# DLRM tower with a two-layer CIN on one core: the third bank's products as 32 matmuls of 32 columns and 8 of 4 in place of 8 of 132

## The reference, cut to what matters

```python
e = jnp.stack([tbl_f[ids[:, f]] for f in range(32)], axis=1)      # 1024 x 32 x 32
x = e
for W in (W0, W1):                                                # 1024 x 128, 4096 x 128
    z = jnp.einsum('bhd,bmd->bhmd', e, x).reshape(b, n * prev, k)
    x = jnp.einsum('bpd,pj->bjd', z, W)
    res.append(x)
z = jnp.sum(jnp.concatenate(res, axis=1), axis=-1)                # 1024 x 256
h = relu(concat([z, dense_ctx]) @ W_top1 + b_top1)
y = relu(h @ W_top2 + b_top2) @ W_top3
```

## Time and profile before

| | |
|---|---|
| median of the runs shown | 376.89 us |
| span of the profiled execution | 597.7 us |
| one tile after the last gather (527.5 to 563.8) | 36.3 us |
| last stretch (563.8 to 597.7) | 33.9 us |
| TensorE passes and weight loads | 3656 and 3656 |
| granted TensorE clock, whole span | 0.800 |

### The profile page before, as it was taken

The page is one execution under the profiler, slowest core; times in us unless marked ns, Lnnn a source line. Parts: engine busy times, 40 slices in busy tenths (PEclk is TensorE's granted clock), DMA queues, the critical chain, the costliest instruction groups (busy, mean ns, idle before and its releaser), DMA issues.

```text
span 597.7 us, 9512 instructions
## 1 busy us (share of the span) xinstructions
PE 412.6 (69%) x3656; PEld 360.8 (60%) x3656; DVE 203.4 (34%) x834; ACT 235.5 (39%) x774; POOL 246.5 (41%) x262
## 2 busy tenths in 40 slices
PE   5512112874257887877788778687787679999988
PEld 4301001653256776766666667577676668989988
DVE  4200000694723333322333233333332235556510
ACT  3300000662175334522343334433452237676641
POOL 6777772547055444544445554544444440000000
PEclk9755555795589877877787888977787779999999
DMA  8100000000000000000000000000000000000000
GB/s 299 45 14 13 13 13 6 11 3 14 2 10 10 8 10 7 10 8 9 9 9 10 10 10 9 11 8 9 8 10 8 8 10 2 2 2 2 2 2 1
DMA packets 10765, 9.66 MB, mean 16 GB/s; under 512 B 4664, under 2 KB 8896, under 8 KB 10720
## 3 DMA queue, kind: packets, MB, share of 16 engines
q0 software_dynamic: 8192, 4.21, 4.8%
q1 hardware_dynamic: 2528, 4.84, 2.3%
HBM read 9.03 MB, written 0.00 MB: 15 GB/s over the span
## 4 chain that ended last, share of the span: by engine, by line
PE 57%; issue 18%; another core or an unknown queue 11%; DVE 7%; ACT 6%; DMA 1%; SPq 0%; ACTq 0%
PE WA L725 20%; PE QB L697 10%; PE PA L687 8%; PE T L710 4%; DVE RT L421 4%; PE M L738 4%; PE M L757 2%; PE ET L674 2%; ACT eblk L285 2%; ACT TS L285 1%; PE PA L639 1%; PE M L764 1%; PE M L748 1%; ACT RT L285 1%
## 5 line engine op out<-in xcount | busy, mean ns | idle before, releaser
L278 POOL DMA_INDIRECT emb<-in_table,rows x256 | 245.8, 960 | 239.0 <-PE ET L674 165.3
L725 PE MATMUL WA<-TS,RX 128*128 128x128 f32 x896 | 127.0, 301 | 1.0 <-ACT TS L285 1.0
L584 DVE COPY TS<-T 32x64 f32<-32x64 f32 x256 | 55.5, 217 | 200.6 <-PE T L710 184.6
L725 PEld LDWEIGHTS WA<-TS,RX 128*128 128x128 f32 x896 | 119.7, 215 | 6.0 <-issue 6.0
L697 PE MATMUL QB<-eblk,zQ 128*64 128x68 f32 x1024 | 69.1, 243 | 74.3 <-issue 74.0
L697 PEld LDWEIGHTS QB<-eblk,zQ 128*64 128x64 f32 x1024 | 49.9, 146 | 89.8 <-issue 85.8
L552 DVE TENSOR_TENSOR zQ<-ET,eT 128x1024 f32<-128x1024 f32 x32 | 39.2, 1225 | 159.0 <-ACT eT L285 158.9
L687 PE MATMUL PA<-eblk,zP 128*128 128x132 f32 x512 | 80.6, 296 | 5.3 <-issue 3.4
L639 PE MATMUL PA<-sym,TS 128*128 128x272 f32 x64 | 29.4, 552 | 74.5 <-issue 47.3
L687 PEld LDWEIGHTS PA<-eblk,zP 128*128 128x128 f32 x512 | 73.4, 212 | 6.3 <-issue 4.9
L285 ACT ACTIVATE eblk<-ET 32x256 f32<-32x256 f32 x128 | 48.6, 380 | 71.0 <-PE ET L674 66.0
(11 more groups left out here) (87 smaller groups left out, 294.1 us busy)
## 6 DMA issues: line engine op xcount, KB each, us to landing
emb<-in_table,rows POOLq DMA_INDIRECT x256
TS<-in_W SPq DMA_DIRECT2D x8, 256.0 KB, 4.3
wt<-in_W_top SPq DMA_DIRECT2D x2, 512.0 KB
y1w<-in_W_rows SPq DMA_DIRECT2D x1, 448.0 KB
TS<-in_W_rows SPq DMA_DIRECT2D x1, 448.0 KB
sym<-in_W_cols SPq DMA_DIRECT2D x1, 264.0 KB, 2.8
TS<-in_W_cols SPq DMA_DIRECT2D x1, 264.0 KB, 3.1
idc<-in_ids SPq DMA_DIRECT2D x1, 128.0 KB, 2.0
```

Source lines behind the costliest of these rows:

```text
L278: eng.indirect_dma_start(emb[par][:, g, :], None, table, bass.IndirectOffsetOnAxis(rows[:, k, g:g + 1], 0))\
L584: eng.tensor_copy(view(ts[32 * q:32 * q + 32, :, :], P * REST + b0, [[4 * P, 2], [P, 4], [1, 8]]), view(src, q, [[C17, 2], [4, 4], [C33, 8 ...
L725: m = eng.matmul(WA[:, 0:P], C[:, kt, :], TS[k % 2][:, slot_of(kt), :], start=(kt == 0), stop=(kt == KT - 1))
```

## The change

`other_triples` now runs per group `g` four matmuls, one for each `q`: the same weights `z3[:, g, :]`, and from `eblk` only the fields with index `q` modulo 4 (32 columns: 4 samples, 2 halves, 4 fields, which lie 4 elements apart). The result goes to partitions `32q` of `T3`, columns `32g` on. Then 8 matmuls of 4 columns each (the inner column of ones) go to partitions 0 to 31. So `T3` already has the partitions of `TS`, and ScalarE brings it there with one copy of 128 x 256 and one of 32 x 32, in slot 1 of the next unit. VectorE's `rest_copies` and the semaphore `t3_also` go.

```diff
-            def rest_copies(u, j):
+            def rest_copies(u):
                 k, unit = divmod(u, UNITS)
-                b0 = 32 * unit + 8 * j
-                src = T3[32 * j:32 * j + 32, :]
+                b0 = 32 * unit
                 eng.wait_ge(t3_made, u + 1)
-                for q in range(NQ):
-                    copy(view(TS[k % 2][32 * q:32 * q + 32, :, :], P * REST + b0, [[4 * P, 2], [P, 4], [1, 8]]),
-                         view(src, q, [[C17, 2], [4, 4], [C33, 8]])).then_inc(t3_also, 1)
-                copy(TS[k % 2][0:32, REST1, b0:b0 + 8], view(src, ONES, [[C33, 8]])).then_inc(t3_also, 1)
+                copy(view(TS[k % 2][:, :, :], P * REST + b0, [[P, 8], [1, 32]]),
+                     view(T3[:, :], 0, [[1, 8], [8, 32]])).then_inc(t3_kept, 1)
+                copy(TS[k % 2][0:32, REST1, b0:b0 + 32], T3[0:32, 8 * 32:9 * 32]).then_inc(t3_kept, 1)
...
-                if r < 2 and u > 0:
-                    rest_copies(u - 1, r + 2)
+                if r == 1 and u > 0:
+                    rest_copies(u - 1)
...
             for u in range(ALL):
-                if u > 0:
-                    for part in range(3):
-                        rest_copies(u - 1, part)
...
             def other_triples(u):
-                wait(eng, t3_kept, 10 * u)
-                wait(eng, t3_also, 10 * u)
-                for x in range(2):
-                    for j in range(NQ):
-                        g = 2 * j + x
-                        at = NQ * C33 * x
-                        m = eng.matmul(T3[32 * j:32 * j + 32, at:at + NQ * C33].rearrange("p (v c) -> p v c", c=C33),
-                                       z3[u % 2][:, g, :], eblk[u % 2][:, g, :, 1:], start=True, stop=True)
+                wait(eng, t3_kept, 2 * u)
+                for g in range(GROUPS):
+                    for q in range(NQ):
+                        some = view(eblk[u % 2][:, :, :, :], EB * g + 1 + q, [[2 * C17, NQ], [C17, 2], [NQ, NQ]])
+                        eng.matmul(T3[32 * q:32 * q + 32, 32 * g:32 * g + 32].rearrange("p (v a b) -> p v a b", v=NQ, a=2),
+                                   z3[u % 2][:, g, :], some, start=True, stop=True)
+                for g in range(GROUPS):
+                    m = eng.matmul(T3[0:32, 8 * 32 + NQ * g:8 * 32 + NQ * g + NQ], z3[u % 2][:, g, :],
+                                   eblk[u % 2][:, g, :, C17], start=True, stop=True)
                 m.then_inc(t3_made, 1)
```

More of the change, by code:

```diff
@@ L173, in dlrm_cin_tower @@
         t3_kept = sem("t3_kept")
-        t3_also = sem("t3_also")
         y2_made = sem("y2_made")
@@ L406, in _ @@
             across_copy(ALL - 1)
-            for j in range(2, NQ):
-                rest_copies(ALL - 1, j)
+            rest_copies(ALL - 1)
             y1_copy(END)
@@ L568, in products @@
                        .then_inc(z_made, 1)
[L570 to L587, removed]
             eng.wait_ge(ids_loaded, 16 * 2)
@@ L620, in _ @@
                     late_sums(u)
-            for part in range(3):
-                rest_copies(ALL - 1, part)
             eng.wait_ge(tower_loaded, 16 * 5)
@@ L721, in second @@
                 if pieces[-1] >= F + HALF:
-                    eng.wait_ge(t3_kept, 10 * UNITS * (k + 1))
-                    eng.wait_ge(t3_also, 10 * UNITS * (k + 1))
+                    eng.wait_ge(t3_kept, 2 * UNITS * (k + 1))
                 for kt in pieces:
```

## The result

The changed kernel takes 384.12 us (median of 4 runs, 383.88 to 384.72) against 376.88 us before (4 runs, 376.80 to 377.10). The ratio is 1.0191, with a 95% interval of 1.0173 to 1.0210: 7.2 us slower. The forecast was 382.0 us, in a range of 375 to 396.

The account below looks back on a forecast made before the run. TensorE was taken as the bound, at 36.3 us a tile. The third bank's added +14.8 us and the -9.4 us from removed copies summed to +5.4 us, 382 us, in a range of 375 to 396.

Parts of the forecast that it names:

- the tile of 36.3 us: The stretch after the gathers, with TensorE busy 34.95 us, taken as each tile's cost; eight make 290 us.
- The third bank, +0.51 us a unit: The T3 matmuls on TensorE were to take 1.09 us in place of 0.58, at 30 ns a pass.
- +14.8: Added TensorE time in us for the T3 matmuls: 0.51 us in each of 29 units.
- The relief, -9.4 us: Time off the path because VectorE's and ScalarE's copies of T3 no longer delay TensorE: 4.7, 1.1 and 3.6 us.
- (1): First tile: two batches of ten VectorE copies ahead of the sums TensorE awaits go, -4.7 us (0 to 4.7).
- (2): First tile: ScalarE's copies of the folded table no longer wait behind five T3 copies, -1.1 us (0 to 2.2).
- (3): Later tiles: the towers' ReLUs no longer stand behind T3 copies on ScalarE, 0.6 us in six tiles, -3.6 us.
- the gathers' pace: Rival: GpSimd's gathers, one per 1.24 us, hide both cost and relief; +1.0 us, 378 us, chance 0.17.
- the columns that lie apart: Rival: moved columns 4 elements apart take twice the time, 56 ns a pass; +17.6 us, 394 us, chance 0.12.
- Issue's pace: Rival: issuing sets the third bank's time at 36 ns a pass; +57 us, 434 us, chance 0.10.
- Faster, under 24 ns a pass: Rival: third-bank passes are cheap enough for the relief to win; at 20 ns a pass 373 us, chance 0.13.
- L757's wait of 0.55 us: Sign in the changed kernel's profile: TensorE's wait for the towers' ReLUs is 0.55 us, in place of 1.35.

Follow-up runs that it names:

- the second profile: The kernel before, unchanged, profiled once more: span 375.7 us, median 377.5 us (1 run).
- the gathers' cover off: Half the gathers from the third tile on: before 369.0 us, changed kernel 383.9 us, before's matmuls with the changed kernel's two copies 354.9 us.

## Why the prediction was right in sign and size, and where it was wrong

**"TensorE is the bound"** holds for the changed kernel (80% of its chain) and failed for the one before, from some 240 us on. The step that failed is the tile of 36.3 us, taken for "what every tile costs". Dropping the 74.0 us of waits as the recorder's was right: the second profile has no such wait. But a tile with gathers takes at least 32 x 1.25 us = 40 us in the end, and that stood in the earlier trace rows beside the 36.3 of the earlier trace rows. I compared the end of all gathers (322 us) with the time and found 14 us to spare. Those 14 us were not there: in the second profile the last gather ends at 333.3, 11.3 us later, its landing takes 1.5 more, and 1.8 lie outside the span. The gathers are late because several of the first take twice as long:

```profile
43.80 2.12 POOL L278 DMA_INDIRECT emb<-in_table,rows  x1 [0.30 <-issue]
...
54.99 0.94 POOL L278 DMA_INDIRECT emb<-in_table,rows  x1 [0.30 <-issue]
...
38.95 6.36 DVE L421 TENSOR_TENSOR RT<-RT,RX 128x64 f32<-128x64 f32 x25
```

The slow ones fall where VectorE adds from and to SBUF; that VectorE is their cause was not tried.

**The third bank, +0.51 us a unit.** It is +0.97, and the step that failed is the price of a 32-column pass, 30 ns by the rule "of weights or of what is moved, whichever is more". That is nearly right for columns side by side (34 ns for four passes in four tiles, bank 1.13 us), and the 4-column passes cost what was forecast (0.59 us for 16 with the change of shape, against 0.61). Columns 16 bytes apart take 60 ns. That was a rival, at 56 ns with +0.93 a unit and a chance of 0.12, and it is shown by three steps of spacing. The +14.8 should have been +29.0.

**The relief, -9.4 us.** With the gathers' cover off it is 14.1. The parts: (1) and (2), the first tile's copies, forecast 5.8, give 7.1 up to the fifth transposes; (3), the towers, forecast 3.6, gives 8.6 - 3.9 = 4.7 us in L757's waits. So the mechanisms were right and each was taken a little small; together they are 11.8 of the 12.7 us in the profiles.

**The sum.** Without the gathers it is 383.9 - 369.0 = +14.9 us, where the forecast had +5.4. The gathers had already cost before 8.8 us, which the changed kernel doesn't pay on top: 14.9 - 8.8 = +6.1. The +7.2 of the result are against a before of 376.9 us, 0.9 less than the 377.8 beside these runs. That the forecast of 382.0 is so close to 384.1 is luck: a bank that costs 14.2 us more than forecast stands against 4.7 us more relief and an unseen wait of 8.8. Two of my rivals together, the gathers' pace and the columns that lie apart, are what happened; I had each as a case of its own and none for both.

**The other rivals.** *Issue's pace* of 36 ns a pass is out: 64 passes ran at 15 ns and, side by side, at 9. The same rows decide against the floor of some 25 ns between matmuls of the Trainium skill (TensorE: Matmul & The Clock Gate, "Wait — 56ns, not 53.3ns?"), where passes go to different column tiles. *Faster, under 24 ns a pass* is out too: even with the columns side by side the bank takes 1.13 us, over the 0.90 at which relief and cost were to balance.

**What was to be seen.** L757's wait of 0.55 us is there (0.56). The tile is 39.3 us in place of 37.5, the bank 1.55 in place of 1.0 to 1.1. "56 in the 32-column part alone of columns that lie apart" was the sign that turned up.

## What to carry to other kernels

Before a price is put on an edit, compare each engine's pace per unit of work, not only the busy shares: here 40 us of gathers a tile stood beside 36.3 us of TensorE, and a relief of 14 us was worth nothing. Where a stream may cover a change, thin out that stream in both kernels; only then does each part show its price (+29.0 and -14.1 us). And when a matmul is cut into parts that pick columns, lay the columns side by side first: the same 64 passes took 0.55 us, 0.61 us at a step of 8 bytes and 0.96 us at one of 16.

## What the runs showed of the hardware beyond that

- Passes of one bank in four column tiles overlap down to 9 ns a pass (64 in 0.55 us); in a single tile nearly all passes of 4 columns begin 31 or 32 ns apart.
- Where the third bank's passes come at 9 to 10 ns while gathers are issued, TensorE's stream of instructions shows holes of up to 0.2 us, with no wait in the profile. All 47 of over 0.1 us begin at one of two places in a gather's 1.25 us (0.40 to 0.53 and 1.16 to 1.25 us after its start); banks that no gather meets have none, and passes at 15 ns show none.
- A gather takes GpSimd 0.94 us and 0.30 between two, whatever the other engines do in the later tiles. In the stretch in which VectorE makes its SBUF sums several take 2.1 us, and in some runs a single one takes 5.6 to 12 us.
- One recorded execution of a kernel may be stretched by 1.59 and the next of the same kernel not at all (597.7 and 375.7 us), so it isn't recording alone that lengthens this kernel. The stretch hid the wait that mattered: in the long one the gathers were never late.
